# A decoder layer on one core: decay rows and masked keys moved to ScalarE, the first weights split later, exponentials from PSUM kept for one pair only

## The chip, the cores and the metric

The kernel runs on one core of a Trainium2 chip. The metric is the device time of the whole program in microseconds (us), as a median of runs. TensorE is called PE, its weight loads PEld, VectorE DVE, ScalarE ACT, GpSimd POOL, and SyncE, which issues every transfer here, SP.

## The reference

The input is 16 sequences of 128 tokens with 256 features, and all arithmetic is in 32-bit floats. Cut to what matters:

```
def layer(x, ctx):                       # x, ctx: (16, 128, 256)
    q, k, v = x@wq+bq, x@wk+bk, x@wv+bv  # 16 heads of 16 features
    a = softmax(q k^T / 4) v             # per head
    x = layernorm(x + a @ wo.T + bo)
    # recurrence over the tokens t, with decays exp(-w), exp(w) per feature
    A = exp(-w) * A + exp(x[t]) * ctx[t]
    B = exp(w) * B + exp(-x[t])
    out[t] = A_before + exp(u + x[t]) * (ctx[t] * B_before + max(t - 1, 0))
    x = layernorm(x + out)
    # eight experts 256 -> 1024 -> 256 with gelu; each takes all 128 tokens
    g = softmax(x @ Wg.T)                # (.., 8)
    y = sum_e g[e] * (gelu(x @ W1[e] + b1[e]) @ W2[e] + b2[e])
    return layernorm(x + y)
```

## The kernel before

**Tiling.** The sequences go in eight pairs p = 0 to 7, of 256 tokens each. The code calls pair 0 `first` and pair 1 `second`. Every 32-bit product is made of three products of a high and a low half (`w_hi`, `w_lo` and so on): ACT copies the high half, and DVE (for some of the first weights POOL) subtracts to get the low half.

**The line.** After a head part the expert layers make one long list, the line, of 512 items (`LINE`). An item is an up unit (x to the hidden layer, 12 matmuls of 256 columns or 6 of 512) or a down unit (12 matmuls of 256 columns). The line visits the experts in turn; pair p joins at visit `JOIN[p]` = 0, 5, 9, 13 and so on and stays for eight visits, so from visit 5 on most visits serve two pairs. Visit 0 has items 0, 1, 2, 3, 5, 6, 8 and 10, visit 5 begins with item 36. Each engine walks through the same line in program order. Behind an up unit ACT applies the gelu (`hidden`, line 906), then copies the high half (`hidden_hi`, line 897), and DVE makes the low half (`hidden_lo`, line 965 by the helper `low`); a down unit waits for that. An up unit waits for the gelu of the unit two before it.

**What hangs on the items.** The steps of the next pair's attention, recurrence and routing hang on items by tables: `EARLY[0]` for pair 1, `EARLY[1]` for pair 2, `STEADY` for the others. An engine does them behind its part of the item. The steps' names are: X (turn x), QK and V (projections), K_COPY and Q_COPY (ACT), K_LOW and Q_LOW (DVE), DIAG (keys masked by head parity, `diagonal`, line 1002), S_u (scores of unit u, four units), M_u (the maxima by row, DVE), E_u (exponentials, ACT), T_u (transposes of the probabilities on PE, their high halves on ACT, low halves on DVE), W_u (weighted values on PE, sums and normalization on DVE), ATT, CTX, WO, NORM1, Y1, XEXP, REC_0 to REC_3 (recurrence), BACK, NORM2, and the routing R_TURN to R_BIAS. The tables `FREE_FIRST` and `FREE` hang one weight piece (256 KB) on nearly every item of visits 0 to 4 and on about every second item of the next three: ACT makes its high half (`split_hi`, line 919), DVE its low half, SP then loads another piece 12 places ahead and stores both halves in DRAM (`w_parts`), from where later visits load them without splitting.

**Exponentials.** For `direct(p)`, p < `DIRECT` = 3, E_u is eight activations of 128 x 128 that read the scores in PSUM with the row's maximum as bias (line 850). For the other pairs DVE adds the negative maximum to each bank of 128 x 512 and writes SBUF in step M_u (line 1044, semaphore `shifted`), and E_u is two activations of 128 x 512 (line 856).

**The head part.** Ahead of the line the lists `FIRST_PE`, `FIRST_ACT`, `FIRST_DVE` and `FIRST_POOL` give each engine's order for pair 0 and the beginning of pair 1. ACT waits there for the constants (`consts_loaded`), then makes high halves of three weight pieces, does E_0 and E_1 of pair 0, splits four more pieces and goes on with E_2. DVE fills `decay_row` (four tensor_scalar of 128 x 128, line 1213) behind M_3 of pair 0 and waits for them. POOL makes the seven low halves (line 1280). `idle_products` are matmuls without use that keep PE at work.

Of the kernel before, what the change touches and what calls it, by code (L numbers as in the profile page):

```python
# [20 lines left out]
def decoder_layer(nc, x, ctx_in, wq, wk, wv, wo, cols, bv, bo, wg, w1, b1, w2, b2, out):  # L21
# [107 lines left out]
    with ExitStack() as ctx:  # L129
# [693 lines left out]
        def _(act):  # L823
# [108 lines left out]
            act.wait_ge(act_setup, 1)  # L932
            for p, s in FIRST_ACT:
                attend(p, s)
                if first(p) and s == V:
# [4 lines left out]
                    nc.scalar.activation(wg_both[:, :, 0, :], wg_raw[:], ACT.Copy).then_inc(act_setup, 1)  # L940
                for i, q in FIRST_SPLIT.get((p, s), []):
                    split_hi(0, i, q)
                if s in ROUTE:
# [458 lines left out]
```

## Time and profile before

| | before |
|---|---|
| median of 3 runs | 947.64 us (947.42 to 948.34) |
| the profiled execution: its own time | 946.98 us |
| its span, first to last instruction | 945.3 us |
| PE busy | 900.6 us (95%) |
| DVE busy | 587.5 us (62%) |
| ACT busy | 588.4 us (62%) |
| POOL busy | 79.0 us (8%) |
| mean granted TensorE clock | 0.98 |

Times of rows are in us from the start of the span. A share of busy time is a mean over stages that have different limits, and matmuls overlap, so a busy PE is not PE at its best pace.

### The profile page before, as it was taken

What the parts mean: (1) busy time and instruction counts of PE and PEld (TensorE: products, weight loads), DVE (VectorE), ACT (ScalarE), POOL (GpSimd) and SP (SyncE); (2) the same over time, 40 slices, a digit from 0 to 9 for tenths busy, and PEclk for the clock granted to TensorE, in tenths of its full rate; (3) what the DMA queues carried; (4) which work ended last, traced back from release to release, by engine and by line L of the source; (5) the groups of instructions that cost most, each with busy time, mean ns of one, the idle gap of its engine ahead of it and who ended that gap; (6) DMA issues with size and microseconds to landing.
All of it is one profiled execution on the core that took longest, in us unless ns stands there. A gap on an engine that the chain in (4) does not pass through costs nothing.

```text
span 945.3 us, 18018 instructions
## 1 busy us (share of the span) xinstructions
PE 900.6 (95%) x6739; PEld 823.0 (87%) x6739; DVE 587.5 (62%) x1214; ACT 588.4 (62%) x1037; POOL 79.0 (8%) x116
## 2 busy tenths in 40 slices
PE   6769798989999999999999999999999999999997
PEld 6659797879988989999988989889988999899997
DVE  6767788656656474765776565665756565433574
ACT  7458986687555655665556765655656665445684
POOL 4220011000110010200120001200101000000000
PEclk9799999999999999999999999999999999999999
DMA  7717999757754454545545555464545555665340
GB/s 238 233 34 256 318 361 372 253 186 248 242 171 157 149 178 152 180 148 176 170 133 170 176 168 167 146 178 146 179 134 171 154 170 166 191 194 164 115 139 12
DMA packets 144694, 172.45 MB, mean 182 GB/s; under 512 B 11208, under 2 KB 110816, under 8 KB 144608
## 3 DMA queue, kind: packets, MB, share of 16 engines
q1 hardware_dynamic: 144608, 171.29, 57.1%
q8 instruction: 55, 0.90, 0.4%
q14 instruction: 31, 0.25, 0.1%
HBM read 135.60 MB, written 35.65 MB: 181 GB/s over the span
## 4 chain that ended last, share of the span: by engine, by line
PE 86%; DVE 6%; ACT 5%; issue 1%; SPq 1%; DMA 0%; POOL 0%; POOLq 0%; DVEq 0%; ACTq 0%
PE down_ps L772 13%; PE down_ps L773 12%; PE down_ps L774 12%; PE up_ps L530 12%; PE up_ps L532 12%; PE up_ps L531 12%; PE bank L597 3%; ACT probs L850 2%; PE bank L574 2%; PE bank L552 1%; PE bank L530 1%; PE bank L532 1%; PE bank L531 1%; PE bank L613 1%; DVE pt_lo L1052 1%
## 5 line engine op out<-in xcount | busy, mean ns | idle before, releaser
L906 ACT ACTIVATE h_all<-up_ps,b_all 128x512 f32<-128x512 f32 (+1 forms) x296 | 182.5, 632 | 262.5 <-PE up_ps L532 253.6
L965 DVE TENSOR_TENSOR h_lo<-h_all,h_hi 128x512 fp32r<-128x512 f32 x256 | 177.4, 693 | 225.0 <-ACT h_hi L897 224.2
L772 PE MATMUL down_ps<-w_hi,h_hi 128*128 128x256 f32 x1024 | 296.3, 289 | 0.3 <-DVE acc L1156 0.3
L773 PE MATMUL down_ps<-w_lo,h_hi 128*128 128x256 f32 x1024 | 291.0, 284 | 0.0
L774 PE MATMUL down_ps<-w_hi,h_lo 128*128 128x256 f32 x1024 | 290.9, 284 | 0.0
L530 PE MATMUL up_ps<-x2t_hi,w_hi 128*128 128x512 f32 (+1 forms) x592 | 222.7, 376 | 0.0
L532 PE MATMUL up_ps<-x2t_hi,w_lo 128*128 128x512 f32 (+1 forms) x592 | 216.9, 366 | 0.0
L531 PE MATMUL up_ps<-x2t_lo,w_hi 128*128 128x512 f32 (+1 forms) x592 | 216.5, 366 | 0.0
L772 PEld LDWEIGHTS down_ps<-w_hi,h_hi 128*128 128x128 f32 x1024 | 196.4, 192 | 8.7 <-issue 0.5
L773 PEld LDWEIGHTS down_ps<-w_lo,h_hi 128*128 128x128 f32 x1024 | 197.0, 192 | 6.7
L774 PEld LDWEIGHTS down_ps<-w_hi,h_lo 128*128 128x128 f32 x1024 | 196.8, 192 | 0.0
L897 ACT ACTIVATE h_hi<-h_all 128x512 fp32r<-128x512 f32 x256 | 162.3, 634 | 38.1 <-PE down_ps L774 33.6
L532 PEld LDWEIGHTS up_ps<-x2t_hi,w_lo 128*128 128x128 f32 x592 | 112.3, 190 | 18.6
L530 PEld LDWEIGHTS up_ps<-x2t_hi,w_hi 128*128 128x128 f32 x592 | 113.1, 191 | 11.9
L531 PEld LDWEIGHTS up_ps<-x2t_lo,w_hi 128*128 128x128 f32 x592 | 113.4, 192 | 10.5
L965 DVE TENSOR_TENSOR w_lo<-w_raw,w_hi 128x512 fp32r<-128x512 f32 x89 | 61.5, 694 | 44.3 <-ACT w_hi L919 44.0
L1247 POOL TENSOR_TENSOR var_eps<-moments,eps_row 128x2 f32<-128x2 f32 x24 | 7.7, 320 | 824.7 <-DVE moments L975 824.7
L919 ACT ACTIVATE w_hi<-w_raw 128x512 fp32r<-128x512 f32 x96 | 60.1, 636 | 0.0
L597 PE MATMUL bank<-ident,probs 128*128 128x128 f32 x232 | 34.3, 297 | 17.8 <-ACT probs L850 17.8
L1156 DVE SCALAR_TENSOR_TENSOR acc<-down_ps,gate,acc 128x256 f32<-128x256 f32 x112 | 47.0, 475 | 3.7 <-PE down_ps L774 3.7
L597 PEld LDWEIGHTS bank<-ident,probs 128*128 128x128 f32 x232 | 29.4, 153 | 20.4 <-ACT probs L850 19.1
L1037 DVE TENSOR_REDUCE neg_max<-bank 128x4 f32<-128x512 f32 x60 | 38.2, 682 | 5.5 <-PE bank L574 5.5
(201 smaller groups left out, 1010.3 us busy)
## 6 DMA issues: line engine op xcount, KB each, us to landing
w_hi<-w_parts SPq DMA_DIRECT2D x200, 256.0 KB, 3.0
w_lo<-w_parts SPq DMA_DIRECT2D x200, 256.0 KB, 3.3
w_raw<-in_w_dram SPq DMA_DIRECT2D x96, 256.0 KB, 4.1
w_parts<-w_hi SPq DMA_DIRECT2D x64, 256.0 KB, 4.0
w_parts<-w_lo SPq DMA_DIRECT2D x64, 256.0 KB, 4.4
x_in<-in_x_dram SPq DMA_DIRECT2D x8, 256.0 KB, 4.0
ctx_sb<-in_ctx_dram SPq DMA_DIRECT2D x8, 256.0 KB, 4.0
out_dram<-acc SPq DMA_DIRECT2D x8, 256.0 KB, 2.6
```

What stands on the lines that cost most here:

```text
L530: nc.tensor.matmul(ps, hi, rhs_hi, start=first, stop=False)
L531: nc.tensor.matmul(ps, hi, rhs_lo, start=False, stop=False)
L532: return nc.tensor.matmul(ps, lo, rhs_hi, start=False, stop=last)
L597: mm = nc.tensor.transpose(by_head(turned(p, u)[i])[:, h, :], probs[:, u % 2, i, h, :], ident[:])
L772: nc.tensor.matmul(ps, hi, w2h[:, c, :], start=c == 0 and j == 0, stop=False, skip_group_check=True)
L773: nc.tensor.matmul(ps, hi, w2l[:, c, :], start=False, stop=False, skip_group_check=True)
L774: mm = nc.tensor.matmul(ps, lo, w2h[:, c, :], start=False, stop=c == FC - 1 and j == PAIR - 1, skip_group_check=True)
L897: nc.scalar.activation(h_hi[:, unit % HALF, :], h_all[:, unit % HALL, :], ACT.Copy).then_inc(h_hi_ready, 1)
L906: a = nc.scalar.activation(h_all[:, unit % HALL, k * wide:(k + 1) * wide], up_ps[unit % 2][:, k * wide:(k + 1) * wide], ACT.Gelu_apprx_tan ...
L919: nc.scalar.activation(piece((w1_hi, w2_hi)[i], i, q), raw(m, i), ACT.Copy)\
L965: return nc.vector.tensor_tensor(dst, src, hi.bitcast(F32), ALU.subtract)
L1156: nc.vector.scalar_tensor_tensor(out=acc[:, p % 2, t, :], in0=by_tile(down_ps[down_banks(n)[a]])[:, t, :], scalar=gate[:, p % 3, t, n % E: ...
```

## The change

1. **Decay rows.** ACT fills `decay_row` with four activations right behind the decays themselves and ahead of its wait for the constants. DVE no longer does it and waits for the semaphore `decay_rows` only at REC_0 of pair 0.
2. **First weights.** The first three high halves now stand ahead of ACT's wait for the constants. The other four stand behind T_3 of pair 0, the end of ACT's share in its attention, and no longer between E_1 and E_2. POOL's low halves and SP's loads and stores follow them in an unchanged order.
3. **Order in the head part.** DVE does V_ADD ahead of M_0. ACT does T_0 and T_1 as early as their inputs allow, around E_2. DIAG_0 and DIAG_1 of pair 1 go from DVE to ACT, as four activations of 128 x 512. PE does S_0 and S_1 of pair 1 ahead of R_TURN of pair 0. ACT calls a gelu on a spare column at R_TURN, so that the table of the gelu is loaded there.
4. **`DIRECT` = 1.** Pairs 1 and 2 go by way of SBUF as the later pairs do: DVE adds, ACT does two activations for each unit.
5. **Steps of pairs 1 and 2 on the line.** E_0 and E_1 of pair 1 go from items 0 and 1 to item 3, with the routing exponential of pair 0, E_2 and E_3 from 10 and 11 to 15; T, W, ATT, WO and NORM1 follow one to five items later, R_TURN one item later. For pair 2 only E_1 and E_3 come one item earlier and some steps move by one.
6. **Bank of x2.** The transposed x2 of pair 1 goes to one bank (bank 0), read by one ACT copy and one DVE subtraction of 128 x 512, and PE no longer waits there for Q_LOW of pair 2.

```diff
@@ back_bank (new)
+        def back_bank(b, c):
+            return by_chunk(bank[0])[:, c, :] if second(b) else bank[c][:, 0:TOK]
@@ tensor: route, part 0
                     pe.wait_ge(x2_ready, b + 1)
-                    if second(b):
-                        pe.wait_ge(q_ready, C * (b + 2))
                     for c in range(C):
                         for t in range(PAIR):
-                            mm = nc.tensor.transpose(bank[c][:, t * S:(t + 1) * S], x2_all[:, b % 2, t, c * P:(c + 1) * P], ident[:])
+                            mm = nc.tensor.transpose(back_bank(b, c)[:, t * S:(t + 1) * S], x2_all[:, b % 2, t, c * P:(c + 1) * P], ident[:])
@@ scalar: attend
+                    if s == DIAGONAL[c] and second(p):
+                        act.wait_ge(k_rest_ready, C * (p + 1))
+                        for a in range(2):
+                            i = nc.scalar.activation(kd[:, :, c, a, :], k_both[:, :, c, :], ACT.Copy, scale=parity[:, a:a + 1])
+                        i.then_inc(kd_ready, 1)
@@ scalar: the head part
             for p, s in FIRST_ACT:
+                if s == R_TURN:
+                    nc.scalar.activation(spare[:], ones[:, 0:1], ACT.Gelu_apprx_tanh)
                 attend(p, s)
                 if first(p) and s == V:
                     ...
+                    act.wait_ge(decay_ready, 1)
+                    act.wait_ge(dve_setup, 1)
+                    for i in range(2):
+                        for c in range(C):
+                            a = nc.scalar.activation(decay_row[:, i, c, :], ones[:], ACT.Copy, scale=decay[:, i, c:c + 1])
+                    a.then_inc(decay_rows, 1)
+                    for i, q in FIRST_SPLIT[(0, V)]:
+                        split_hi(0, i, q)
                     act.wait_ge(consts_loaded, 16 * CONSTS)
@@ vector
-                    if s == DIAGONAL[c]:
+                    if s == DIAGONAL[c] and not second(p):
                         diagonal(p, c)
                 if s == RECUR[0]:
+                    if first(p):
+                        dve.wait_ge(decay_rows, 1)
-                if first(p) and s == DECAY_AT:
-                    dve.wait_ge(decay_ready, 1)
-                    for i in range(2):
-                        for c in range(C):
-                            a = nc.vector.tensor_scalar(decay_row[:, i, c, :], ones[:], decay[:, i, c:c + 1], None, ALU.mult)
-                    a.then_inc(decay_rows, 1)
-                    dve.wait_ge(decay_rows, 1)
@@ tables
 EARLY = [
-    {E_0: 0, E_1: 1, T_0: 2, T_1: 3, W_0: 5, W_1: 6, X_BIAS: 6, S_2: 8, M_2: 8, S_3: 8, M_3: 8, E_2: 10, E_3: 11, T_2: 14, T_3: 15, W_2: 17, W_3: 18, ATT: 20, CTX: 20,
-     WO: 22, NORM1: 24, Y1: 26, XEXP: 26, REC_0: 26, REC_1: 27, REC_2: 28, REC_3: 28, BACK: 31, NORM2: 31, R_TURN: 33,
-     R_LOGITS: 35, R_MAX: 36, R_GATE: 41, R_GATE_T: 50, R_BIAS: 51},
+    {E_0: 3, E_1: 3, X_BIAS: 6, T_0: 7, T_1: 8, W_0: 10, W_1: 11, S_2: 13, M_2: 13, S_3: 13, M_3: 13, E_2: 15, E_3: 15, T_2: 17, T_3: 18, W_2: 20, W_3: 21,
+     ATT: 22, CTX: 22, WO: 23, NORM1: 25, Y1: 26, XEXP: 26, REC_0: 27, REC_1: 28, REC_2: 29, REC_3: 29, BACK: 31, NORM2: 32, R_TURN: 34,
+     R_LOGITS: 36, R_MAX: 37, R_GATE: 41, R_GATE_T: 50, R_BIAS: 51},
...
-FIRST_ACT = ([(0, s) for s in (K_COPY, V, E_0, E_1, E_2, T_0, T_1, E_3, T_2, T_3)]
-             + [(1, X), (0, ATT), (0, CTX), (1, K_COPY), (0, XEXP), (1, Q_COPY), (0, R_TURN)])
-FIRST_DVE = ([(0, s) for s in (K_LOW, DIAG_0, Q_LOW, K_LOW_1, Q_LOW_1, DIAG_1, M_0, V_ADD, M_1, M_2, M_3, T_0, T_1, W_0, W_1, T_2, T_3, W_2)]
+FIRST_ACT = ([(0, s) for s in (K_COPY, V, E_0, E_1, T_0, E_2, T_1, E_3, T_2, T_3)]
+             + [(1, X), (0, ATT), (0, CTX), (1, K_COPY), (0, XEXP), (1, Q_COPY), (1, DIAG_0), (1, DIAG_1), (0, R_TURN)])
+FIRST_DVE = ([(0, s) for s in (K_LOW, DIAG_0, Q_LOW, K_LOW_1, Q_LOW_1, DIAG_1, V_ADD, M_0, M_1, M_2, M_3, T_0, T_1, W_0, W_1, T_2, T_3, W_2)]
...
-FIRST_ROUTE = {0: [1], 1: [2, 3], 6: [4], 8: [5]}
-FIRST_SPLIT = {(0, V): [(0, 0), (0, 1), (0, 2)], (0, E_1): [(0, 3), (1, 0), (1, 1), (1, 2)]}
+FIRST_ROUTE = {0: [1], 1: [2], 3: [3], 8: [4], 10: [5]}
+FIRST_SPLIT = {(0, V): [(0, 0), (0, 1), (0, 2)], (0, T_3): [(0, 3), (1, 0), (1, 1), (1, 2)]}
...
-DIRECT = 3
+DIRECT = 1
```

## Rows read from the trace of the kernel before

**Rows 1.** Stretch, length; busy PE, PEld, DVE, ACT, POOL; granted clock, DMA share, GB/s.

```profile
58.30:100.00 41.70, 29.75 (x272) 29.00 (x269) 24.62 (x51) 37.42 (x82) 5.14 (x6) 0.91 0.63 212
100.00:150.70 50.70, 46.42 (x386) 45.48 (x385) 45.80 (x92) 40.00 (x81) 6.40 (x8) 0.94 1.00 342
150.70:216.00 65.30, 59.09 (x454) 52.49 (x453) 43.13 (x84) 47.98 (x98) 2.48 (x3) 0.95 0.75 253
...
286.00:900.00 614.00, 613.76 (x4468) 556.19 (x4466) 357.12 (x740) 364.71 (x576) 37.02 (x54) 1.00 0.53 162
```

**Rows 2.** Timeline of PE: start, duration, group, idle time before it and its releaser.

```profile
71.18 1.97 PE L597 MATMUL bank<-ident,probs 128*128 128x128 f32 x8 [7.45 <-ACT probs L850]
...
94.18 0.28 PE L772 MATMUL down_ps<-w_hi,h_hi 128*128 128x256 f32 x1
94.30 0.28 PE L773 MATMUL down_ps<-w_lo,h_hi 128*128 128x256 f32 x1
...
99.20 1.96 PE L597 MATMUL bank<-ident,probs 128*128 128x128 f32 x8 [4.50 <-ACT probs L850]
...
143.39 0.88 PE L687 MATMUL bank<-ident,x 128*128 128x128 f32 x4 [2.64 <-DVE q_lo L988]
...
166.79 1.33 PE L597 MATMUL bank<-ident,probs 128*128 128x128 f32 x8 [3.23 <-ACT probs L850]
...
198.50 1.97 PE L597 MATMUL bank<-ident,probs 128*128 128x128 f32 x8 [2.61 <-ACT probs L850]
```

**Rows 3.** The stretch in which PE comes back from its longest wait.

```profile
70.00:76.00 6.00, 4.82 (x26) 4.83 (x27) 2.63 (x5) 5.97 (x14) 0.00 (x0) 0.55 0.37 128
```

**Rows 4.** Timeline of ACT on the line: start, duration, group.

```profile
67.55 1.28 ACT L887 ACT_TABLE_LOAD   x1
68.85 0.21 ACT L887 ACTIVATE route_exps<-logits 128x16 f32<-128x16 f32 x1
...
76.19 0.86 ACT L906 ACTIVATE h_all<-up_ps,b_all 128x256 f32<-128x256 f32 x2
76.91 1.12 ACT L863 ACTIVATE pt_hi<-bank 128x512 f16<-128x512 f32 x2
77.86 0.68 ACT L919 ACTIVATE w_hi<-w_raw 128x512 fp32r<-128x512 f32 x1
...
281.25 2.19 ACT L856 ACTIVATE probs<-probs 128x512 f32<-128x512 f32 x4
```

**Rows 5.** Chain of work that ended last, head part: start, duration, step.

```profile
9.56 3.40 DMA b_raw<-in_b_dram
...
13.51 1.56 ACT w_hi L919 x3
15.07 2.00 ACT probs L850 x8
...
26.05 2.50 DVE pt_lo L1052 x4
28.59 1.97 PE up_ps L597 x8
...
58.37 0.32 PE up_ps L530
```

**Rows 6.** Timeline of DVE: start, duration, group.

```profile
21.25 4.77 DVE L1213 TENSOR_SCALAR decay_row<-ones,decay 128x128 f32<-128x128 f32 x4
...
112.75 0.29 DVE L1062 TENSOR_TENSOR att<-pv_sum,inv_sum 128x128 f32<-128x128 f32 x1
...
141.72 0.73 DVE L982 TENSOR_SCALAR x<-y,moments,rstd 128x256 f32<-128x256 f32 x2 [1.09 <-POOL rstd L1250]
...
275.59 1.28 DVE L1044 TENSOR_TENSOR probs<-bank,neg_max 128x512 f32<-128x512 f32 x2
```

**Rows 7.** Timeline of POOL, the low halves of the first weights.

```profile
19.76 8.62 POOL L1280 TENSOR_TENSOR w_lo<-w_raw,w_hi 128x512 fp32r<-128x512 f32 x7
```

More of the change, by code:

```diff
@@ L183, in decoder_layer @@
         y1 = sb("y1", [P, PAIR, D])
+        spare = sb("spare", [P, 1])
         stats = sb("stats", [P, PAIR, 6])
@@ L881, in route @@
                 if part == 0:
-                    for c in range(C):
+                    if second(b):
+                        act.wait_ge(x2t_ps, C * (b + 1))
+                        nc.scalar.activation(x2t_hi[:, :, b % 3, :], by_chunk(bank[0]), ACT.Copy).then_inc(x2t_hi_ready, C)
+                    for c in range(0 if second(b) else C):
                         act.wait_ge(x2t_ps, C * b + (c + 1))
@@ L940, in _ @@
                     nc.scalar.activation(wg_both[:, :, 0, :], wg_raw[:], ACT.Copy).then_inc(act_setup, 1)
-                for i, q in FIRST_SPLIT.get((p, s), []):
-                    split_hi(0, i, q)
+                if s != V:
+                    for i, q in FIRST_SPLIT.get((p, s), []):
+                        split_hi(0, i, q)
                 if s in ROUTE:
@@ L1112, in route @@
                 if part == 0:
-                    for c in range(C):
+                    if second(b):
+                        dve.wait_ge(x2t_hi_ready, C * (b + 1))
+                        low(x2t_lo[:, :, b % 3, :], by_chunk(bank[0]), x2t_hi[:, :, b % 3, :]).then_inc(x2t_ready, C)
+                    for c in range(0 if second(b) else C):
                         dve.wait_ge(x2t_hi_ready, C * b + (c + 1))
@@ L1208, in _ @@
                                                    op0=ALU.mult, op1=ALU.add).then_inc(dve_setup, 1)
-                if first(p) and s == DECAY_AT:
-                    dve.wait_ge(decay_ready, 1)
-                    for i in range(2):
-                        for c in range(C):
-                            a = nc.vector.tensor_scalar(decay_row[:, i, c, :], ones[:], decay[:, i, c:c + 1], None, ALU.mult)
-                    a.then_inc(decay_rows, 1)
-                    dve.wait_ge(decay_rows, 1)
                 if s in ROUTE:
@@ L1334 @@
 EARLY = [
-    {E_0: 0, E_1: 1, T_0: 2, T_1: 3, W_0: 5, W_1: 6, X_BIAS: 6, S_2: 8, M_2: 8, S_3: 8, M_3: 8, E_2: 10, E_3: 11, T_2: 14, T_3: 15, W_2: 17, W_3: 18, ATT: 20, CTX: 20,
-     WO: 22, NORM1: 24, Y1: 26, XEXP: 26, REC_0: 26, REC_1: 27, REC_2: 28, REC_3: 28, BACK: 31, NORM2: 31, R_TURN: 33,
-     R_LOGITS: 35, R_MAX: 36, R_GATE: 41, R_GATE_T: 50, R_BIAS: 51},
-    {X: 24, X_LOW: 25, X_BIAS: 27, QK: 28, K_COPY: 28, Q_COPY: 28, K_LOW: 30, Q_LOW: 31, DIAG_0: 33, V: 32, V_ADD: 34, V_SPLIT: 35,
-     S_0: 37, M_0: 37, S_1: 37, M_1: 37, DIAG_1: 40, E_0: 41, E_1: 42, T_0: 44, T_1: 45, W_0: 48, W_1: 49, S_2: 53, M_2: 53, S_3: 53, M_3: 53, E_2: 57, E_3: 58,
+    {E_0: 3, E_1: 3, X_BIAS: 6, T_0: 7, T_1: 8, W_0: 10, W_1: 11, S_2: 13, M_2: 13, S_3: 13, M_3: 13, E_2: 15, E_3: 15, T_2: 17, T_3: 18, W_2: 20, W_3: 21,
+     ATT: 22, CTX: 22, WO: 23, NORM1: 25, Y1: 26, XEXP: 26, REC_0: 27, REC_1: 28, REC_2: 29, REC_3: 29, BACK: 31, NORM2: 32, R_TURN: 34,
+     R_LOGITS: 36, R_MAX: 37, R_GATE: 41, R_GATE_T: 50, R_BIAS: 51},
+    {X: 25, X_LOW: 26, X_BIAS: 27, QK: 29, K_COPY: 29, Q_COPY: 29, K_LOW: 30, Q_LOW: 32, DIAG_0: 33, V: 32, V_ADD: 35, V_SPLIT: 36,
+     S_0: 38, M_0: 38, S_1: 38, M_1: 38, DIAG_1: 40, E_0: 41, E_1: 41, T_0: 44, T_1: 45, W_0: 48, W_1: 49, S_2: 53, M_2: 53, S_3: 53, M_3: 53, E_2: 57, E_3: 57,
      T_2: 60, T_3: 61, W_2: 64, W_3: 65, ATT: 68, CTX: 69, WO: 71, NORM1: 73, Y1: 76, XEXP: 76, REC_0: 76, REC_1: 77, REC_2: 79,
@@ L1355 @@
 FIRST_PE = ([(0, s) for s in (X, QK, V, S_0, S_1, S_2, S_3, T_0, T_1, W_0, T_2, W_1, T_3, W_2)]
-            + [(1, X), (0, W_3), (0, ATT), (0, CTX), (0, WO), (1, QK), (0, Y1), (1, V), (0, BACK), (0, R_TURN), (1, S_0), (1, S_1)])
-FIRST_ACT = ([(0, s) for s in (K_COPY, V, E_0, E_1, E_2, T_0, T_1, E_3, T_2, T_3)]
-             + [(1, X), (0, ATT), (0, CTX), (1, K_COPY), (0, XEXP), (1, Q_COPY), (0, R_TURN)])
-FIRST_DVE = ([(0, s) for s in (K_LOW, DIAG_0, Q_LOW, K_LOW_1, Q_LOW_1, DIAG_1, M_0, V_ADD, M_1, M_2, M_3, T_0, T_1, W_0, W_1, T_2, T_3, W_2)]
+            + [(1, X), (0, W_3), (0, ATT), (0, CTX), (0, WO), (1, QK), (0, Y1), (1, V), (0, BACK), (1, S_0), (1, S_1), (0, R_TURN)])
+FIRST_ACT = ([(0, s) for s in (K_COPY, V, E_0, E_1, T_0, E_2, T_1, E_3, T_2, T_3)]
+             + [(1, X), (0, ATT), (0, CTX), (1, K_COPY), (0, XEXP), (1, Q_COPY), (1, DIAG_0), (1, DIAG_1), (0, R_TURN)])
+FIRST_DVE = ([(0, s) for s in (K_LOW, DIAG_0, Q_LOW, K_LOW_1, Q_LOW_1, DIAG_1, V_ADD, M_0, M_1, M_2, M_3, T_0, T_1, W_0, W_1, T_2, T_3, W_2)]
              + [(0, W_3), (1, X_LOW), (0, ATT), (0, WO), (0, NORM1), (1, K_LOW), (0, REC_0), (0, REC_1), (0, REC_2), (0, REC_3), (1, V_ADD),
-                (0, BACK), (1, DIAG_0), (0, NORM2), (1, Q_LOW), (0, R_TURN), (1, DIAG_1), (1, M_0), (1, M_1)])
+                (0, BACK), (1, Q_LOW), (0, NORM2), (0, R_TURN), (1, M_0), (1, M_1)])
 FIRST_POOL = [(0, V_SPLIT), (0, X_BIAS), (0, WO), (0, BACK), (1, V_SPLIT)]
-FIRST_ROUTE = {0: [1], 1: [2, 3], 6: [4], 8: [5]}
-FIRST_SPLIT = {(0, V): [(0, 0), (0, 1), (0, 2)], (0, E_1): [(0, 3), (1, 0), (1, 1), (1, 2)]}
+FIRST_ROUTE = {0: [1], 1: [2], 3: [3], 8: [4], 10: [5]}
+FIRST_SPLIT = {(0, V): [(0, 0), (0, 1), (0, 2)], (0, T_3): [(0, 3), (1, 0), (1, 1), (1, 2)]}
 FIRST_SPLIT_LOW = {(0, X_BIAS): [(0, 0), (0, 1), (0, 2), (0, 3), (1, 0), (1, 1), (1, 2)]}
-SETUP_AT, DECAY_AT = ATT, M_3
-DIRECT = 3
+SETUP_AT = ATT
+DIRECT = 1
 PROJECTIONS = (1, 0, 2, 3)
```

## The prediction

> **What bounds the kernel now.** I read the busy times by stretch first. From 286 to 900 us PE is busy for 613.76 of 614.00 us at full clock [rows 1]: no change of the other engines shortens that part, and the pairs from the fourth on aren't touched. Ahead of it PE is not full: 29.75 of 41.70 us from 58.30 to 100, 46.42 of 50.70 to 150.7, 59.09 of 65.30 to 216 [rows 1]. So the time is the start of the line, plus PE's work on it, plus PE's waits in its first 160 us.
>
> The timeline of PE names the waits. Four are for the exponentials of pairs 1 and 2, ahead of the transposes T_0 and T_2: 7.45, 4.50, 3.23 and 2.61 us, 17.8 together; one of 2.64 us stands ahead of R_TURN of pair 1, put down to Q_LOW of pair 2 [rows 2]. A wait costs more than its length: from 70 to 76 us the granted clock is 0.55, so between 1.2 GHz and little over it, while PE is busy for 4.82 us [rows 3], which is about 4.82 x 0.45 = 2.2 us of lost work. The shorter waits lose less; I take 7 for the four, 1.6 each for the last two. Together the four cost some 25 us.
>
> The other part is the head, ahead of the first up unit at 58.37 [rows 5]. Its chain goes over the landing of the constants (9.56 + 3.40 = 12.96), three weight splits on ACT (1.56), E_0 from 15.07, DVE's low halves from 26.05, and the transposes T_2 at 28.59 [rows 5]. DVE's four decay rows take 4.77 us right before 26.05 [rows 6].
>
> **The head, part by part.** Prices: a small exponential 0.25 (8 in 2.00) [rows 5]; two pt_hi copies 0.95, a gelu of a single pair 0.72, both from start to start; a split or copy of 128 x 512 is 0.52, from four exponentials in 2.19 less the overlap [rows 4]; a DVE operation on 128 x 512 is 0.60 (two in 1.28, with the same overlap) [rows 6].
>
> The decay rows on ACT aren't in the trace. The nearest row is the 128 x 128 exponential, 0.25, so 1.0 for four (1.9 if each cost a whole 128 x 512 operation, and never below nothing). They and the three splits now stand in ACT's wait for the constants, which covers them: the weights are issued ahead of the constants in SP's queue. E_0 starts at about 13.6, 1.45 earlier; if the weights land last, up to 1.5 comes back. V_ADD ahead of M_0 costs 0.15 on M_0 with slack behind it, and lets S_1 go at once.
>
> Now E_0 and E_1 take 4.0 to 17.6; PE turns four heads in 1 us at the low clock and ACT copies both halves by 20.1; E_2 to 22.1; T_1's copies to 23.1; DVE, free of the decay rows, has the last low half at 23.8. T_2 starts on PE at 23.9 in place of 28.59: **4.7 us**. Behind it W_1, T_3 and all of the chain to 58.37 is the same work in the same order, so the line starts at 53.7. With the clock up at T_2 and T_3 it could be 1 more; the bounds are 3.2 and 5.7.
>
> What moved behind: the four splits (2.1) fall in ACT's idle time after T_3. POOL's last four low halves (8.62 / 7 = 1.23 each) [rows 7] run from 30 to 35; its next work, the root for NORM1, comes at 38. SP issues behind them four loads and fourteen stores, and then ctx of pair 1; the first stores land near 40, the last near 52, and ACT first needs one at item 1, near 59. The masked keys on ACT: four of 0.52 to 0.60, in idle time between Q_COPY and R_TURN, nothing. The gelu table (1.28 [rows 4]) was hidden behind the first up unit and is hidden again. S_0 and S_1 of pair 1 ahead of R_TURN: under a microsecond of PE in its wait for x2, nothing.
>
> **The line to R_TURN of pair 1.** I count from the start of the line, 58.3 before. A unit is twelve matmuls of 0.12 [rows 2], so 1.43.
>
> ACT. Up to item 3 it has four gelus, three copies and three splits, and the second up unit only ends at 4.0, so the table load begins at 8.5; routing exponential and four exponentials of 0.52 end at 12.0. Of table loads pair 1 now has four and not eight: 5.1 us less ACT time at 1.28. T_0's transposes go at 12.9, as early as before, but with seven units done in place of three or four.
>
> The Trainium skill ("ScalarE: Activation LUTs", What ACT_TABLE_LOAD costs) gives 1283 ns for the load and about 1380 ns of drain at each switch; by it four switches fewer were worth 10.6 us and not 5.1. The load at 67.55 ends at 68.83 and the next activation starts at 68.85 [rows 4], so no drain is to be seen here.
>
> DVE. By the end of W_3 (112.75 + 0.29, that is 54.7 after the line's start) [rows 6] it has worked 24.6 us to 100 and some 12 of 13 behind it [rows 1], so 36.6, and idled 18, mostly behind ACT in the two blocks of exponentials. New work up to that point: eight adds of 0.60, 4.8; less one masked key pair, 1.3; and, as W_3 stands three items later, three more splits and one or two hidden halves, 2.9. That is 43.0. I walked its queue against ACT's and find 7 us of waits left: 2.6 for the routing exponential and the split behind the exponentials, 1.9 for the next split (a table load and a gelu lie ahead of it), 1.8 ahead of T_2, the rest small. So W_3 ends at 49.9 (before 54.7).
>
> PE. To item 22 it has 23 units, routing, T_0 to T_3, W_0 to W_3 and two scores, 40.9 us, and these new waits: 1.1 for gate_t (ACT is full), 0.4 for the biased x2, 2.1 ahead of S_2 (which needs W_1's sums, late on DVE), 0.5 ahead of T_2. It comes to ATT at 45.4 and waits there for W_3: 4.5 us. That is the new long wait. Behind ATT wait WO, the down units and all of pair 1's chain.
>
> From W_3's end to the end of x2's normalization (141.72 + 0.73) DVE needed 29.4 us [rows 6] and was nearly full, 45.80 of 50.70 in the stretch [rows 1]. Two items' low halves fewer lie in between (about 2), and Q_LOW's wait and the second small operation go (about 1): 26.3. So x2 is ready at 76.2, turned at 76.6, and by then PE has done item 34. Before, R_TURN began at 143.39 and the down unit of item 34 came behind it at the low clock, to 146.7, that is 88.4 [rows 2]. Gain **11.8**. From below, 7 (if ACT delays DVE as it did before); from above 22, all the waits of pair 1 with their clock.
>
> **Pair 2.** ACT's two blocks shrink from 4.4 to 2.1, table loads stay as they are. E_0 is ready at about 162.7 of the old time, and PE had come to T_0 at 166.79 - 3.23 = 163.56 [rows 2]: no wait. M_u grow by 2.4 a block on DVE, which idles 22 of 65.3 us there [rows 1] and has three items until E_0. Both waits go: 3.23 + 2.61 + 3.2 for the clock = **9.0**; from below 5.8, from above 10.2 (2.2 each).
>
> The one bank for x2 saves 0.14 on each of ACT and DVE, counted above. Transfers: the share is 1.00 at 342 GB/s from 100 to 150.7 [rows 1]. The bytes of the line to there, 41.7 x 212 + 50.7 x 342 = 26.2 MB, need 76.6 us at that rate, and the new length is 79 or so: just hidden, and a floor for this stretch.
>
> **The sum.** 4.7 + 11.8 + 9.0 = 25.5. The profiled execution took 946.98 (945.3 of span and 1.7 around it); less 25.5 it is 921.5. The median lies 0.66 above it: 922.1, given as 922. The tail doesn't change.
>
> **Rivals.** (a) As above, 917 to 927: 0.50.
> (b) PE's waits nearly vanish, as the exponentials come in time and DVE isn't late: gain 31 to 36, so 911 to 916. For it: DVE's waits were behind ACT, which gets 5 + 8 us of pair 1 and 2 back. Against: DVE's 43 us of work to W_3. 0.13.
> (c) DVE or the transfers set pair 1's part: DVE is late from M_2 on, each hidden half with it, and ATT waits 8 to 10 us. The line's gain to item 34 is then 4 to 7, the whole 16 to 19: 928 to 932. For it: DVE 0.90 busy from 100 on. 0.23.
> (d) POOL beside DVE. DVE's decay rows took 1.19 each while POOL made its low halves (19.76 to 28.38) [rows 6, 7], though they are a quarter of a bank each. POOL's last four now run beside W_2 and W_3 of pair 0, whose normalization reads two small tiles in SBUF; held by up to 1.2 each they put 2.4 back on the chain: 924.5. 0.10, within (a)'s range. The Trainium skill ("GPSIMD Engine Reference", Specifications) says that the two engines contend where DVE runs in a two-port mode or reads two SBUF inputs; the decay rows fit the first, the normalization would be the second.
> (e) Slower: with more and shorter waits PE stays at the low clock for most of the line's beginning. Each us of work done there costs another. It decides from 25.5 us of such work on; PE has about 70 to item 34. With 32 of them, 954. Against: 0.91 and 0.94 were granted with the longer waits [rows 1]. 0.04.
>
> A measurement of this kernel tells about 0.2%, 1.9 us, from no change. Faster by more than that: (a) to (d), 0.95 with rounding; within it 0.01; slower 0.04. The range: 913 to 932 takes in (a), (d), most of (b) and (c).
>
> **What would show it.** Right: the first up unit near 53.7; T_2 of pair 0 near 23.9; no wait of PE for probs beyond 1 us; ATT of pair 1 with a wait of 3 to 6 us for DVE; R_TURN of pair 1 near 130; from pair 3 on every row as before, about 25 us earlier. Wrong: a start later than 55.5 (weights landing last, or POOL beside DVE); waits for `shifted` or for hidden halves at M_2; a DMA as the last releaser of a split; a low granted clock without a wait ahead of it.

## The result, and the profile of the changed kernel

| | before, same session | after |
|---|---|---|
| median | 947.53 us (946.62 to 948.34, 4 runs) | 935.26 us (931.94 to 936.19, 4 runs) |
| profiled execution: own time, span | 946.98, 945.3 us | 934.52, 932.8 us |
| granted clock, mean | 0.98 | 0.988 |

The ratio is 0.9864, 95% interval 0.9838 to 0.9891: the change makes the kernel 1.4% faster. Forecast were 922 us and 913 to 932, so the sign was right and the size was not: 12.5 us of the profiled execution in place of 25.5.

By stretches, with the columns of [rows 1]: from the start of the line to W_3 of pair 1, to S_0 of pair 2, the rest of pair 2, and the steady part.

```profile
54.36:107.00 52.64, 44.45 (x411) 42.50 (x412) 43.60 (x85) 41.88 (x83) 4.99 (x6) 0.97 0.87 296
107.00:150.00 43.00, 38.13 (x297) 36.68 (x295) 34.80 (x72) 26.91 (x53) 10.13 (x10) 0.92 0.95 322
150.00:203.30 53.30, 50.78 (x400) 44.93 (x399) 42.36 (x83) 41.44 (x70) 0.00 (x0) 1.00 0.74 249
273.30:887.30 614.00, 614.00 (x4468) 556.30 (x4466) 356.86 (x740) 364.51 (x576) 37.36 (x54) 1.00 0.52 162
```

The last line is PE's full part, as in [rows 1]: nothing changed there. Ahead of it PE is still not full. From W_3's end to the end of x2's normalization in pair 1, first before, then after (columns as in rows 1):

```profile
113.04:142.45 29.41, 26.84 (x224) 26.43 (x224) 26.68 (x56) 22.78 (x46) 4.22 (x6) 1.00 1.04 361
```

```profile
106.63:137.15 30.52, 26.88 (x199) 26.47 (x200) 24.09 (x51) 19.68 (x39) 4.59 (x6) 0.89 0.90 301
```

DVE works 2.6 us less there than before and yet the stretch is 1.1 us longer: DVE idles 6.4 us where it idled 2.7. The timeline of PE, its first instructions behind a wait:

```profile
24.47 1.09 PE L602 MATMUL up_ps<-ident,probs 128*128 128x128 f32 x8 [2.27 <-DVE pt_lo L1074]
...
32.87 0.66 PE L557 MATMUL bank<-ident,att 128*128 128x128 f32 x4 [1.36 <-DVE att L1084]
...
82.89 0.51 PE L579 MATMUL bank<-kd,q_hi 32*128 32x256 f32 x8 [1.82 <-DVE att L1084]
...
106.69 0.66 PE L557 MATMUL bank<-ident,att 128*128 128x128 f32 x4 [4.01 <-DVE att L1084]
...
131.04 0.66 PE L682 MATMUL bank<-ident,mix 128*128 128x128 f32 x4 [3.12 <-DVE mix L1123]
...
147.48 0.51 PE L579 MATMUL bank<-kd,q_hi 32*128 32x256 f32 x8 [0.86 <-POOL v_all L1289]
...
159.91 0.39 PE L775 MATMUL down_ps<-w_hi,h_hi 128*128 128x256 f32 x1 [1.21 <-DVE acc L1183]
...
188.11 0.36 PE L775 MATMUL down_ps<-w_hi,h_hi 128*128 128x256 f32 x1 [1.30 <-DVE acc L1183]
```

T_2 of pair 0 stands at 24.47 in place of 28.59 [rows 5], and the four waits for exponentials of [rows 2], 17.8 us, are gone. In their place are shorter ones that DVE releases: at S_2 (1.82), ATT (4.01) and BACK (3.12) of pair 1 and twice for `acc` (1.21, 1.30). One of 0.86 at S_0 of pair 2 is put down to POOL; m_combo shows below that it is DVE's too. The timeline of DVE:

```profile
30.30 1.25 DVE L1084 TENSOR_TENSOR att<-pv_sum,inv_sum 128x128 f32<-128x128 f32 x1
...
106.34 0.29 DVE L1084 TENSOR_TENSOR att<-pv_sum,inv_sum 128x128 f32<-128x128 f32 x1
...
112.19 0.69 DVE L1093 TENSOR_TENSOR y<-bank,x_bo 128x512 f32<-128x512 f32 x1 [2.48 <-PE bank L537]
...
121.07 0.69 DVE L987 TENSOR_TENSOR w_lo<-w_raw,w_hi 128x512 fp32r<-128x512 f32 x1 [1.99 <-ACT w_hi L930]
...
130.30 0.69 DVE L1123 TENSOR_TENSOR mix<-mix,inc_a 128x512 f32<-128x512 f32 x1
...
132.90 0.68 DVE L1126 TENSOR_TENSOR y<-bank,y 128x512 f32<-128x512 f32 x1
...
136.42 0.73 DVE L1004 TENSOR_SCALAR x<-y,moments,rstd 128x256 f32<-128x256 f32 x2 [0.59 <-POOL rstd L1270]
```

From these rows, where the time went:

| part | forecast | measured |
|---|---|---|
| start of the line | 4.7 | 58.30 - 54.36 = 3.94 |
| pair 1, to the end of item 39 (156.50 before, 150.06 after; the forecast counted to R_TURN) | 11.8 | 98.20 - 95.70 = 2.50 |
| pair 2 and the rest (the last two additions of pair 3 at 275.59 [rows 6], now at 262.92) | 9.0 | 12.67 - 6.44 = 6.23 |
| sum | 25.5 | 12.67 |

Within pair 1, counted from the line's start: W_3 ended 52.27 (54.7 before, forecast 49.9), and x2 was normalized 82.79 (84.15 before, forecast 76.2).

### The profile page after: what moved, and what is told of

Same layout as the page of the kernel before. It is cut to its first block, busy times and chain, and to the rows that moved or that the text cites. A ratio compares the mean times of both kernels' runs of the same rounds, so it can differ in the third digit from the quotient of the medians.

```text
span 932.8 us, 17982 instructions
## 1 busy us (share of the span) xinstructions
PE 898.2 (96%) x6739; PEld 819.7 (88%) x6739; DVE 590.0 (63%) x1221; ACT 577.7 (62%) x993; POOL 80.2 (9%) x116
## 4 chain that ended last, share of the span: by engine, by line
PE 83%; DVE 6%; ACT 4%; issue 1%; POOL 1%; POOLq 0%; ACTq 0%; DVEq 0%
PE down_ps L775 12%; PE up_ps L535 12%; PE down_ps L776 12%; PE down_ps L777 12%; PE up_ps L537 12%; PE up_ps L536 12%; PE bank L602 2%; PE bank L579 1%; PE bank L557 1%; PE bank L535 1%; PE bank L537 1%; PE bank L536 1%; DVE w_lo L987 1%; ACT h_all L917 1%; DVE acc L1183 1%
## 5 line engine op out<-in xcount | busy, mean ns | idle before, releaser
L1074 DVE TENSOR_TENSOR pt_lo<-bank,pt_hi 128x512 f16<-128x512 f32 x58 | 37.2, 683 | 4.1 <-ACT pt_hi L871 2.6
```

## The experiments

Eighteen runs. The table gives for each the median, the ratio to the kernel before with its interval, and five marks of its profiled execution, read from the timelines of PE and DVE: the start of the line, and from there the ends of W_3, of the recurrence (`mix`) and of x2's normalization for pair 1, and the start of S_0 of pair 2. The start moves by 1.4 us from run to run with one and the same code. The marks behind it agree within 0.1 us where the code up to them is the same, but for two things: W_3 stands at 52.3 or at 50.8, and the marks behind it move with it, for a reason that c_fill shows; and p_pool_hold has its `mix` 0.8 late. So they tell more than medians do.

| run | median | ratio (95%) | start | W_3 | mix | x2 | S_0 |
|---|---|---|---|---|---|---|---|
| before | 947.53 | | 58.30 | 54.74 | 77.47 | 84.15 | 94.20 |
| after | 935.26 | 0.9864 (0.9838, 0.9891) | 54.36 | 52.27 | 76.63 | 82.79 | 93.12 |
| a_again | 934.47 | 0.9869 (0.9851, 0.9887) | 54.58 | 52.25 | 76.64 | 82.81 | 93.12 |
| b_rec26 | 935.91 | 0.9886 (0.9865, 0.9907) | 55.30 | 52.28 | 74.30 | 81.67 | 92.00 |
| c_fill | 932.76 | 0.9855 (0.9836, 0.9874) | 55.26 | 50.68 | 73.53 | 79.70 | 90.02 |
| d_fill_rec26 | 931.70 | 0.9839 (0.9822, 0.9856) | 55.57 | 50.68 | 71.18 | 79.07 | 89.40 |
| e_head | 942.71 | 0.9955 (0.9940, 0.9969) | 53.66 | 54.67 | 77.41 | 84.09 | 94.14 |
| f_pair2_psum | 939.18 | 0.9922 (0.9905, 0.9939) | 54.83 | 52.30 | 76.65 | 82.82 | 93.15 |
| g_dve_extra | 933.72 | 0.9860 (0.9846, 0.9875) | 55.16 | 50.78 | 75.17 | 81.34 | 91.67 |
| h_low_late | 936.10 | 0.9887 (0.9872, 0.9902) | 57.53 | 50.77 | 75.13 | 81.30 | 91.63 |
| i_hi_first | 932.23 | 0.9854 (0.9840, 0.9869) | 55.28 | 50.79 | 75.22 | 81.39 | 91.71 |
| j_turn33 | 931.37 | 0.9842 (0.9828, 0.9857) | 55.72 | 50.69 | 71.19 | 79.08 | 88.71 |
| k_less_dve | 936.03 | 0.9890 (0.9870, 0.9911) | 55.48 | 50.79 | 75.22 | 81.39 | 92.74 |
| l_best | 931.24 | 0.9842 (0.9826, 0.9858) | 54.95 | 50.70 | 71.20 | 79.09 | 89.90 |
| m_combo | 929.37 | 0.9808 (0.9793, 0.9823) | 55.28 | 50.72 | 71.22 | 79.14 | 87.78 |
| n_combo_pool | 931.32 | 0.9825 (0.9809, 0.9840) | 56.27 | 50.71 | 71.21 | 79.15 | 87.78 |
| o_dve_late | 936.54 | 0.9879 (0.9861, 0.9897) | 55.24 | 52.28 | 76.69 | 84.64 | 94.97 |
| p_pool_hold | 936.13 | 0.9877 (0.9860, 0.9894) | 56.68 | 52.31 | 77.39 | 83.57 | 93.89 |
| q_hold_setup | 929.28 | 0.9806 (0.9792, 0.9819) | 53.52 | 50.71 | 71.21 | 79.14 | 87.77 |
| r_combo_again | 930.00 | 0.9816 (0.9802, 0.9829) | 55.34 | 50.68 | 71.19 | 79.08 | 87.72 |

**a_again.** The changed kernel itself.

> The changed kernel once more, unchanged, beside the three variants. Expected 935 us, from 932 to 936 as in its first runs.

**The clock behind the new waits (c_fill).** The idle matmuls write a bank that is written anew behind them.

```diff
+ if u == 2 and second(p): idle_products(bank[1], 8)     # ahead of S_2
+ if second(p): idle_products(bank[3], 18)               # ahead of ATT
+ if second(p):                                          # ahead of BACK
+     pe.wait_ge(exps_ready, p + 1); idle_products(bank[0], 13)
```

> Idle matmuls fill three waits of PE in pair 1, about 0.21 us each at full clock: 8 ahead of S_2, 18 ahead of ATT, 13 ahead of BACK. Nothing that computes is changed. Theory A (PE's low clock behind these waits lengthens the chain): the clock stays up, items 23, 24, 32 and 33 take their full-clock times, 930 to 932 us. Rival B (the amount of DVE's work, or the transfers, bounds pair 1): a gain below 1, 934 to 935.

x2 is 3.1 us earlier and S_0 too, as theory A has it; the median, 932.76, is 0.8 above its range. The two parts can be told apart: W_3 comes 1.59 earlier, and from W_3 to y another 1.52 (5.56 us in the changed kernel, 4.04 with the matmuls; y starts at 112.19 and 109.98). From y to the recurrence's end nothing changes (18.8 in both), and from there to x2 neither (6.2). The stretches in which PE comes back from the waits at S_2 and ATT, in the changed kernel (columns as in rows 1):

```profile
84.00:86.00 2.00, 2.00 (x11) 2.00 (x11) 2.00 (x4) 0.00 (x0) 0.00 (x0) 0.50 1.08 385
...
107.00:110.00 3.00, 3.00 (x21) 3.00 (x19) 1.61 (x3) 1.60 (x3) 0.00 (x0) 0.64 1.07 376
```

and in c_fill:

```profile
84.00:86.00 2.00, 2.00 (x35) 1.87 (x32) 2.00 (x5) 0.00 (x0) 0.00 (x0) 1.00 1.06 350
...
107.00:110.00 3.00, 3.00 (x27) 3.00 (x27) 1.40 (x3) 2.76 (x7) 0.00 (x0) 1.00 1.07 386
```

PE counts as busy all the time in all four rows; what differs is the granted clock, 0.50 being 1.2 GHz and 1.00 being 2.4, and with it the matmuls done. There is a surprise in the table: g, h, i and k have W_3 at 50.8 without any idle matmuls there. They have the same wait of 1.8 us at S_2, but the clock didn't fall behind it. The same window in i_hi_first:

```profile
84.00:86.00 2.00, 2.00 (x34) 1.87 (x34) 2.00 (x4) 0.00 (x0) 0.00 (x0) 1.00 1.07 374
```

So a wait of 1.8 us costs 1.5 us of clock in some executions and nothing in others; in all eight profiled executions with idle matmuls there the clock stayed up. It probably has a large part in why one kernel's runs lie between 931.94 and 936.19: the run of 931.94 has a mean granted clock of 0.993, the other three 0.988. Only profiled executions show where the clock fell.

**The order of the recurrence (b_rec26, d_fill_rec26).**

```diff
- REC_0: 27, REC_1: 28, REC_2: 29, REC_3: 29
+ REC_0: 26, REC_1: 27, REC_2: 28, REC_3: 28
```

> REC_0 to REC_3 of pair 1 stand one item earlier (26, 27, 28, 28), so that REC_0 comes ahead of the weight split of item 26, whose high half ACT makes only behind XEXP's exponentials. Theory A (the chain of pair 1 bounds the line, not the amount of anybody's work): DVE's wait of 2.0 us ahead of w_lo at 121 us leaves the chain, the mix is 2 to 3 us earlier, 932 to 933.5 us. Rival B (the amount of DVE's work bounds pair 1): 935 within 0.7. Rival C (the transfers bound it): as B.

> Both edits, the idle matmuls and REC_0 to REC_3 one item earlier. Theory A: 928 to 930 us. Rival B: 934 to 935.

DVE's wait of 1.99 us at 121.07 is gone, in its place stands one of 0.85 for ACT's `inc_b`, and `mix` is 2.34 earlier in b than in a, 2.35 in d than in c. But x2 gains only 1.14 and 0.63, so theory A is half right at most. By the medians neither forecast of it came true: b's 935.91 shows no gain (its line started 0.7 later than a's, and one of its five runs took 938.74), and d's 931.70, 1.06 below c's, is above 928 to 930. The timeline of DVE in b_rec26:

```profile
128.91 0.69 DVE L1123 TENSOR_TENSOR mix<-mix,inc_a 128x512 f32<-128x512 f32 x1
...
131.33 0.87 DVE L1010 SCALAR_TENSOR_TENSOR k_both<-bank,bqk,k_both 128x256 f32<-128x256 f32 x2
...
132.71 0.68 DVE L1126 TENSOR_TENSOR y<-bank,y 128x512 f32<-128x512 f32 x1
```

In the changed kernel y starts 1.91 us behind the end of `mix`, here 3.11, and DVE has no idle time in between: low halves and K_LOW of pair 2 stand ahead of y in its queue.

**Where DVE is full (g_dve_extra, o_dve_late).** The same three reductions at two places; nothing reads what they write.

```diff
+ if second(p):                 # g: right behind att_lo; o: right behind REC_3's addition
+     for i in range(3): nc.vector.tensor_reduce(idle_out[:, i], ones[:]..., AX_X, ALU.add)
```

> The changed kernel with three more VectorE reductions of 128x512 (0.6 us each, 1.8 in all) right behind att_lo of pair 1; nothing reads them. Latency theory (a chain over several engines bounds that stretch): they fall into DVE's 2.5 us wait ahead of y, at most 0.3 us longer, 934.5 to 935.5. Rival (the amount of DVE's work): 1.8 us longer, 936.3 to 937.5.

> The changed kernel with three more VectorE reductions (1.8 us) right behind REC_3 of pair 1. If VectorE's queue is full from the recurrence to x2: 1.8 us on x2 and the end, 936.3 us. If a latency sets that stretch as it did ahead of y: 934.5 to 935.

Ahead of y they cost nothing: g against i, which had the same clock there, has the marks 75.17 and 75.22, 81.34 and 81.39. (g's 933.72 is below even the latency forecast, as its clock stayed up at S_2.) Behind the recurrence they cost all that they take, in the timeline of DVE of o_dve_late:

```profile
131.24 0.69 DVE L1124 TENSOR_TENSOR mix<-mix,inc_a 128x512 f32<-128x512 f32 x1
131.85 1.87 DVE L1127 TENSOR_REDUCE idle_out<-ones 128x4 f32<-128x512 f32 x3
...
139.14 0.74 DVE L1005 TENSOR_SCALAR x<-y,moments,rstd 128x256 f32<-128x256 f32 x2 [0.59 <-POOL rstd L1274]
```

x2 comes 84.64 - 82.79 = 1.85 us later, and the median is 936.54. So both theories hold, each in its own part: latency ahead of y, DVE's amount of work behind the recurrence's end to x2 and S_0 (94.97 - 93.12 = 1.85). Between the two no run adds work. The changed kernel's timeline of DVE has its wait of 1.99 us at 121.07 and then none until the 0.59 for the root at 136.42.

**Behind x2 (j_turn33, k_less_dve, and the logits in m_combo).** j stands on d_fill_rec26, k on the changed kernel.

```diff
- R_TURN: 34,   Q_LOW: 32, DIAG_0: 33        # of pair 1, of pair 2
+ R_TURN: 33,   Q_LOW: 33, DIAG_0: 34        # j
- if s == DIAGONAL[c] and second(p):         # on ACT
+ if s == DIAGONAL[c] and p in (1, 2):       # k: on ACT, no longer on DVE
```

> With the idle matmuls and the recurrence one item earlier, and x2 of pair 1 turned behind item 33, not 34, with Q_LOW and DIAG_0 of pair 2 an item later, so that x2t_lo stands ahead of them in VectorE's queue. Theory (VectorE's queue between x2 and x2t_lo sets item 36): x2t_lo 1.2 to 1.7 us earlier, 930 to 931 us beside 931.7. Rival (VectorE's amount of work up to S_0 sets it): 931.7.

> The changed kernel with pair 2's masked keys on ScalarE too, in its wait of 6.8 us: 0.8 us less on VectorE ahead of x2t_lo. If VectorE's work sets the stretch behind x2: 0.8 us faster, 933.7. If not: 934.5.

In j x2t_lo ends 81.28 behind the line's start in place of 83.05, 1.77 earlier, but S_0 only 0.69, and the median is 931.37, between the two forecasts. k is no gain, 936.03 and above both forecasts: with 0.8 us less to do, DVE has x2t_lo done 86.25 behind the start, against 85.37 in i. The masked keys take 1.33 us on ACT and stand there ahead of a weight split, and DVE waits for the split (timeline of DVE, k_less_dve):

```profile
139.83 0.69 DVE L987 TENSOR_TENSOR w_lo<-w_raw,w_hi 128x512 fp32r<-128x512 f32 x1 [1.58 <-ACT w_hi L930]
```

ACT's wait of nearly 7 us was over before its queue came to them.

**Pair 2's exponentials and `acc` (f_pair2_psum, i_hi_first).**

```diff
- return p < DIRECT
+ return p == 0 or p == 2                    # f
+ late = [(p, s) for p, s in steps(FIRST_ITEM[n] + k) if p == 2 and s in EXPS or s == R_GATE and p == 1]
+ # i: done on ACT behind the item's splits and hidden_hi, not ahead of them
```

> The changed kernel, but with pair 2's exponentials straight from PSUM again (16 small ones per block, no shift adds for it). Theory (the exponentials' time on ScalarE is what the waits at T_0 and T_2 were for): both waits return, 3 us each less the one on acc that goes, 938 to 941 us. Rival (the waits went because everything else in pair 2 moved): 934.5 to 936.

> Items 41 and 57 on ScalarE: the gelu, then the weight split and h_hi, and only then the four exponentials of pair 2 (in the changed kernel the exponentials stand between the gelu and h_hi). Theory: VectorE's h_lo no longer waits 3.3 us for h_hi, so acc behind it is in time and PE's two waits for acc (1.21 and 1.30 us) go: 2.5 us faster than the changed kernel, 932 us. Rival (PE then waits as long for the later exponentials at T_0 and T_2): 934.5.

f: PE waits 2.22 and 2.11 us at T_0 and T_2 again, and 0.8 to 1.0 for `acc`; it is 3.9 to 4.7 us slower than the changed kernel's two medians. The small exponentials were what those waits were for. i: from the end of item 39 to the end of item 63 41.60 us, not 43.41; the second wait for `acc` is gone, but the first is still 0.95. So the second wait came from the order on ACT: DVE's `acc` stands behind h_lo, h_lo waited 3.29 us for h_hi, and ACT copied that behind four exponentials. The first did not: h_hi is 4 us earlier in i, and this `acc` is only 0.8 earlier there, with no wait of DVE's in the timeline from 151 us up to it. Ahead of it stands the amount of DVE's own work, the maxima and additions of pair 2 among it. That i's median, 932.23, meets the forecast is in part luck: its profiled execution kept the clock at S_2, and beside g, which kept it too, i is 1.5 us faster.

**The head (e_head, h_low_late, p_pool_hold, q_hold_setup).**

```diff
  EARLY, FIRST_ROUTE, DIRECT = 3 and x2's banks as before                        # e
- FIRST_SPLIT_LOW = {(0, X_BIAS): [... all seven]}
+ FIRST_SPLIT_LOW = {(0, X_BIAS): [first three], (0, WO): [last four]}            # h
+ if (i, q) == (0, 3): pool.wait_ge(att_ready, UNITS)     # p; n and q on m_combo
+ SETUP_AT = WO                                            # q alone, was ATT
```

> Only the part of the change ahead of the line: decay rows on ScalarE, the four late weight splits behind the attention, setup order. The line's tables, the exponentials of pairs 1 and 2 from PSUM and the four banks for x2 are those of before. Theory (parts add up): the line starts 3.9 us earlier as in the changed kernel, and the rest is as before: 943 to 943.7 us. Rival (the earlier start is taken back by pair 1, as its transfers are no earlier): 945 to 947.

> GpSimd makes the last four low halves of the first weights behind NORM1's root, not beside W_2 and W_3 of pair 0. Theory (GpSimd beside VectorE held W_2 and W_3 by 1.2 us): the two att take 0.29 each, ATT's transposes start 1.2 earlier, 933.3 to 934.5 if the scans of pair 0, now beside GpSimd, keep their times (1.37 and 0.69 us); if they are held as much, no gain or some loss, 934.5 to 937.

> The changed kernel with GpSimd's last four low halves held until W_3 of pair 0 is done. Contention theory: both att of W_2 and W_3 take 0.29 us, the line starts 1.2 us earlier, 933.3 us. Rival: held elsewhere, 934.5.

> m_combo with GpSimd's last four low halves held until W_3 of pair 0 is done (not beside W_2 and W_3, and over before NORM1's root). If GpSimd beside VectorE cost the head 1.2 us: 1.2 below m_combo. If the line's first units then wait for those halves, or att_lo and y are held instead: no gain.

> n_combo_pool with VectorE's preparation of the routing weights' and biases' low halves behind y's moments, in the wait for NORM1's root, where GpSimd's four low halves are nearly over. If the contention was what cost: the line starts 21.5 us behind ATT as in the changed kernel and ATT comes 1.2 earlier, 1.2 below the combined kernel. If something else is held in its place: no gain.

e: the head alone is worth 4.1 us (946.84 less 942.71, same session), a little more than forecast, and behind the line's start its marks are those of the kernel before within 0.1 us: the parts add up. None of h, p and n gains: 936.10, as its second forecast has it; 936.13, above both forecasts; and 931.32, 1.95 above m. In h both `att` take 0.29 us and ATT's transposes come 8.29 behind T_2, against 9.57 in b and 9.56 in m with T_2 at the same clock: 1.28 us had been lost beside POOL. How much is lost depends on how the two queues meet: in e the two `att` took 0.56 and 0.52 us, and from T_2 to the line's start it was 29.23 us; in the changed kernel 1.25 and 0.50, and 29.89. But h loses more elsewhere; its timeline of DVE:

```profile
40.05 2.61 DVE L1004 TENSOR_SCALAR y<-y,moments,rstd 128x256 f32<-128x256 f32 x2 [1.10 <-POOL rstd L1270]
...
44.09 2.20 DVE L1030 TENSOR_TENSOR_SCAN inc_b<-decay_row,inc_b 128x128 f32<-128x128 f32 x4 [0.64 <-issue]
```

They take 0.73 and 1.37 us in the changed kernel. p moves the harm to the preparation of the biases (timeline of DVE):

```profile
35.39 1.44 DVE L1231 TENSOR_SCALAR b_raw<-b_raw,third 24x256 f32<-24x256 f32 x1
...
36.92 1.34 DVE L1234 SCALAR_TENSOR_TENSOR b_all<-b_hi,third,b_raw 24x256 fp32r<-24x256 f32 x1
```

They take 0.33 and 0.47 us in the changed kernel; in p y has to wait for them in DVE's queue, and starts at 38.19. Only q, which keeps both away from POOL, has the time: the line starts 28.83 behind T_2, against 30.10 in r_combo_again. Its median, 929.28, is only 0.7 below that of r in the same session, where 1.2 was forecast. In the profiled execution, at least, the clock fell behind PE's wait of 2.08 us for `acc` and took it back; the one of its four runs with a mean granted clock of 0.997 took 927.45. First q_hold_setup, then r_combo_again, with the same wait (columns as in rows 1):

```profile
156.00:158.00 2.00, 2.00 (x13) 2.00 (x11) 1.79 (x3) 2.00 (x5) 0.00 (x0) 0.51 1.08 371
```

```profile
158.00:160.00 2.00, 2.00 (x17) 1.91 (x16) 2.00 (x4) 2.00 (x5) 0.00 (x0) 1.00 1.06 371
```

The Trainium skill ("SBUF — State Buffer", SBUF: two separate sides) says that GpSimd and VectorE share a port pair, which goes to one of them for a whole instruction, VectorE's needing it in a two-port mode or with two inputs in SBUF. The rows agree: each DVE instruction above (the 2.61 is for two) is longer by less than one POOL instruction, about 1.27 us (5.07 for four in p), and xt_lo and att_lo, which read PSUM, keep their 0.68 and 0.69 beside it.

**All together (l_best, m_combo, r_combo_again).** l is j with k's and i's edits; m is j with i's and this one:

```diff
- R_LOGITS: 36, R_MAX: 37,
+ R_LOGITS: 36, R_MAX: 36,
```

> All that helped or should: idle matmuls in three waits, the recurrence one item earlier, x2 turned behind item 33, pair 2's masked keys on ScalarE, h_hi ahead of pair 2's exponentials. If the gains add: 1 + 0.8 + 2.5 below 931.7, so 927 to 928.5. If one limit takes another's place: 929.5 to 931.

> Idle matmuls, recurrence one item earlier, x2 turned behind item 33, h_hi ahead of pair 2's exponentials, and the logits of pair 1 reduced at item 36, not 37. By VectorE's queue, the logits' reduction releases S_0 of pair 2 (it frees the bank that the scores go to), so PE's 0.9 us at S_0 goes: 931.4 less 2.1 less 0.9, 928.4 us. If S_0 waits for GpSimd: 929.3.

> The combined kernel m_combo once more, beside q_hold_setup: 929.4 us, 928.5 to 931.

l, 931.24, was no better than j and above both forecasts, as k's edit stands in it: its S_0 is at 89.90, j's at 88.71. In m S_0's wait is gone and S_0 0.93 earlier than in j: the scores go to the bank that holds the logits, and that reduction stood behind two low halves in DVE's queue; S_0 started right behind it. The profile had named POOL there. The median is the 929.3 that was forecast if S_0 waits for POOL, but not for that reason: the wait went as forecast, and one of 2.08 us for `acc` came. 929.37 and 930.00 us are 1.9% and 1.8% below the kernel before, and m's interval lies wholly below that of the changed kernel.

## Why the prediction was wrong

**Right.** PE's full part is as before. Decay rows on ACT 1.28 us for four (1.0), E_0 at 13.80 (13.6), T_2 at 24.47 (23.9), the line at 54.36 (53.7). The four waits for exponentials are gone. S_2 waits 1.82 us (2.1), gate_t 0.58 (1.1). ATT waits 4.01 us for DVE (4.5), but that is luck: PE came to it at 48.3 behind the line's start (45.4; the terms given for it add up to 45.0) and W_3 ended at 52.27 (49.9), both over 2 us late.

**The head, 0.8 too much.** T_2 itself came 0.6 late: E_0 0.2, and ACT had T_0's copies at 20.55, not 20.1. Behind it rival (d) was a part of the truth. POOL beside W_2 and W_3 cost 1.06 us (29.89 from T_2 to the line's start, 28.83 in q; up to 1.28 in other executions), and the full clock at T_2 gave 0.9 back.

**Pair 1, 9.3 too much: the step that failed.** It is "From W_3's end to the end of x2's normalization ... DVE needed 29.4 us [rows 6] and was nearly full", and the 26.3 us made of it. The 29.4 us were the time that went by; DVE worked 26.68 of them. The forecast took some 3 us of work off that time, as if DVE's work set it. The work did shrink, to 24.09 us, but the stretch took 82.79 - 52.27 = 30.5 us, 4.2 more than forecast. The runs show in its place:
- Ahead of y no engine's amount of work sets it, but a chain over PE, ACT and DVE: 1.9 us more on DVE were absorbed there (g). The chain was longer by PE's low clock behind ATT, 1.5 us (c), which I had charged to the old waits and not to the new one.
- Moving REC_0 one item later put it behind a weight split that ACT makes only behind XEXP's exponentials: 1.99 us of wait, worth 0.6 to 1.1 at x2 (b, d).
- Only behind `mix` does more work on DVE lengthen it by as much (o). The remaining 2.1 us stay open: with both repairs, in d, the stretch is still 79.07 - 50.68 = 28.4 us, and DVE works 24.20 of them:

```profile
106.25:134.64 28.39, 27.26 (x216) 26.22 (x216) 24.20 (x51) 19.80 (x39) 4.61 (x6) 1.00 0.97 329
```

W_3 itself was 2.4 late: 1.5 by the clock behind S_2's wait (c, g), and 0.8 is left, which no run locates. With the 4.2 of the stretch that makes 6.6 of the 9.3. Another 1.2 came as PE, at the low clock behind BACK, reached R_TURN only at 138.76, 84.40 behind the start and 1.6 behind x2, where 0.4 was forecast (0.1 in c_fill and in b_rec26, whose clock was up there); the last 1.5 came behind it, at x2t_lo and S_0, which j and m shortened by 1.77 and 0.93.

**Pair 2, 2.8 too much.** The waits and their clock did go; in their place came the two waits for `acc`, 2.5 us, which the forecast has no term for. The second, 1.3 us, came by the order on ACT (i); the first stands behind DVE's own work.

**The rivals.** The result lies above (c) too, which had blamed the amount of DVE's work or the transfers. The transfers aren't it: in c the same transfers let x2 come 3.1 us earlier. (e)'s mechanism was real, but small: some 3 us in pair 1, not 32. I gave it all or nothing and did not put a part of it into the sum. That is one reason why the range was short at 932, but not the whole: with the clock held up, c still has 932.76. The rest is pair 1's chain: even (c) had a gain of 4 to 7 there. (The parts of (c), 4.7, 4 to 7 and 9.0, add up to 17.7 to 20.7 and not to 16 to 19.)

Open: the remaining 0.8 of W_3 and 2.1 us behind it; and what decides whether the clock falls behind a wait of 1.8 to 2.1 us.

## What to carry to other kernels

When long waits are replaced by short ones, charge the clock to each new wait as well as crediting it for the old ones, and cover the surest ones with idle matmuls. Before calling a stretch bound by an engine's amount of work, set the engine's busy time beside the time that goes by, look for its idle time and ask who ends it; three spare instructions at the suspected place settle it. A step moved by one item changes its neighbours in three queues: read what each engine has ahead of it there, above all table switches and copies that another engine's next step needs.

## What was not expected of the hardware

- The same wait of PE, 1.8 us, was followed by 1.2 GHz (0.50 to 0.62 granted in 2 us) in six of the profiled executions without idle matmuls there (after, a, b, f, o, p) and by 2.4 GHz (1.00) in four (g, h, i, k). The wait of 2.08 us for `acc` was followed by a fall in n and q and by none in m and r. Behind the wait of 4.0 us at ATT the clock fell in all ten. The Trainium skill ("TensorE: Matmul & The Clock Gate", Part 1) says of the rise at a kernel's start that its moment varies from run to run. These rows show the like for the fall behind a wait.
- POOL loses beside DVE as well: its cast of 128x512 took 0.64 us while DVE reduced banks of PSUM (a_again, 54.59) and 2.24 us while DVE made low halves (143.48).
- Two instructions with small tiles, 24x256, went from 0.33 and 0.47 us to 1.44 and 1.34 beside POOL. They lost 1.11 and 0.87 us, as much as an `att` of 128x128 (0.96): the price goes by what is left of POOL's instruction of 1.27 us rather than by their own size.
